# The first group's expert layer laid between the second group's attention steps, in an order written out by hand

## The reference

```
h = token(x, mask, rel_dist)            # embeddings, masked neighbour sums, norm, silu, two weights
h = h + attention(layernorm(h))         # phases, cosines and sines, cumulative sums over the tokens
h = h + experts(layernorm(h))

def experts(x):                         # E = 8 experts, the best K = 2 of each token are summed
    gate_scores = x @ Wg + bg
    _, idx = top_k(gate_scores, 2)
    mask = one_hot(idx, E).sum(-2)
    h = gelu(einsum('td,edh->teh', x, W1) + b1)     # hidden width 128
    y = einsum('teh,ehd->ted', h, W2) + b2
    return einsum('ted,te->td', y, mask)
```

## Time and profile before

| | |
|---|---|
| device time, 3 runs | 214.52, 214.59, 216.08 us; median 214.59 |
| the profiled execution: its time, its span | 213.43 us, 211.7 us |
| PE busy | 147.7 us, 70% of the span |
| PE weight loads busy | 90.8 us, 43% |
| DVE busy | 131.1 us, 62% |
| ACT busy | 73.9 us, 35% |
| POOL busy | 35.6 us, 17% |
| mean granted clock of TensorE | 0.778 of full speed |
| chain that ended last, by engine | PE 43%, DVE 34%, issue 9%, DMA 5%, ACT 5%, POOL 2% |

### The profile page before, as it was taken

How to read it: one execution, slowest core, us unless ns; L and a number is a source line. 1 busy time by engine, 2 the same in 40 slices (tenths; PEclk the granted TensorE clock), 3 DMA queues, 4 the chain that set the end, 5 groups by cost and what they waited for, 6 DMA issues and landing times.

```text
span 211.7 us, 2099 instructions
## 1 busy us (share of the span) xinstructions
PE 147.7 (70%) x690; PEld 90.8 (43%) x690; DVE 131.1 (62%) x342; ACT 73.9 (35%) x122; POOL 35.6 (17%) x52
## 2 busy tenths in 40 slices
PE   0889858029279694499581054877479989979992
PEld 0543524024175512458561053766454454534340
DVE  2659995789942898998879995388673005101011
ACT  2010511252233640784840230323063462444541
POOL 2031500346000472241402330000000000000000
PEclk9999979758857955558997555799555896799998
DMA  5999600000000000000000000000000000101011
GB/s 145 345 386 377 262 5 25 0 0 0 0 0 0 0 0 0 0 5 2 0 0 5 0 0 0 0 5 0 0 0 0 0 3 0 25 0 25 0 25 25
DMA packets 7042, 8.80 MB, mean 42 GB/s; under 512 B 2388, under 2 KB 4436, under 8 KB 7032
## 3 DMA queue, kind: packets, MB, share of 16 engines
q1 hardware_dynamic: 7032, 8.68, 12.2%
HBM read 8.15 MB, written 0.52 MB: 41 GB/s over the span
## 4 chain that ended last, share of the span: by engine, by line
PE 43%; DVE 34%; issue 9%; DMA 5%; ACT 5%; POOL 2%; SPq 1%; DVEq 0%; POOLq 0%; ACTq 0%
PE bank L900 8%; PE bank L884 6%; DMA dist_sb<-in_dist 5%; PE bank L885 4%; PE bank L861 2%; PE bank L640 2%; DVE dist_sb L988 2%; PE bank L705 2%; PE bank L698 2%; PE bank L702 2%; DVE proj L1059 2%; PE bank L707 2%; DVE invpos L993 2%; PE bank L690 2%; PE bank L754 1%
## 5 line engine op out<-in xcount | busy, mean ns | idle before, releaser
L586 ACT ACTIVATE hid<-bank 128x512 f32<-128x512 f32 x32 | 18.1, 596 | 23.3 <-PE bank L885 22.2
L900 PE MATMUL bank<-hid,ffn_sb 128*64 128x512 f32 x64 | 18.9, 676 | 0.0
L1271 DVE TENSOR_TENSOR h<-bank,h 128x256 f32<-128x256 f32 x4 | 1.7, 425 | 27.0 <-PE bank L909 27.0
L884 PE MATMUL bank<-xp,w1hi 128*128 128x512 f32 x32 | 16.6, 520 | 1.0 <-ACT xp L570 1.0
L885 PE MATMUL bank<-xp,w1lo 96*128 96x512 f32 x32 | 14.6, 455 | 0.0
L884 PEld LDWEIGHTS bank<-xp,w1hi 128*128 128x128 f32 x32 | 7.0, 220 | 14.4 <-ACT hid L586 8.1
L988 DVE TENSOR_TENSOR dist_sb<-dist_sb,mask_in 128x1024 f32<-128x1024 f32 x8 | 9.5, 1232 | 4.0 <-POOL mask_in L325 4.0
L698 PE MATMUL bank<-late_sb,proj 128*128 128x8 f32 x16 | 3.7, 364 | 10.8 <-ACT proj L469 10.8
L656 PE MATMUL bank<-early_sb,vk 128*128 128x128 f32 x8 | 2.2, 435 | 12.9 <-DVE vk L1038 12.9
L830 PE MATMUL bank<-early_sb,sq_c 128*128 128x2 f32 x16 | 2.9, 304 | 11.8 <-ACT sq_c L545 11.8
L640 PE MATMUL bank<-dist_sb,neigh 128*64 128x512 f32 x32 | 11.1, 775 | 0.0
(11 more groups left out here) (246 smaller groups left out, 369.4 us busy)
## 6 DMA issues: line engine op xcount, KB each, us to landing
dist_sb<-in_dist SPq DMA_DIRECT2D x4, 1024.0 KB, 10.8
mask_in<-in_mask SPq DMA_DIRECT2D x4, 256.0 KB, 10.0
ffn_sb<-in_ffn SPq DMA_DIRECT2D x1, 813.0 KB, 10.9
fold_sb<-in_folded SPq DMA_DIRECT2D x1, 772.0 KB, 12.1
late_sb<-in_late SPq DMA_DIRECT2D x1, 728.5 KB, 11.6
out<-h SPq DMA_DIRECT2D x8, 64.0 KB, 1.7
early_sb<-in_early SPq DMA_DIRECT2D x1, 391.0 KB, 3.2
mask_in<-in_mrows SPq DMA_DIRECT2D x1, 128.0 KB, 2.4
```

What stands on the lines that cost most here:

```text
L586: nc.scalar.activation(hid[:, at % HB], bank[hid_bank[at % 3]][:, :], ACT.Gelu).then_inc(S["hid_set"], 1)
L884: nc.tensor.matmul(o, w1hi[:, e * HID:(e + 1) * HID], xp1[g][:, toks], start=True, stop=False)
L900: mm = nc.tensor.matmul(bank[2][j * D:(j + 1) * D, :], K["e_w2"][:, (e + j) * D:(e + j + 1) * D], hid[:, (at + j) % HB], start=False, stop ...
```

## The change

It is one new order, one more empty step in X, and other banks and a later place for group 0's turns:

- `ORDER`: out3 of group 0's core, C0.8, C0.9 and X0.1 now come before or just after Q1.4 (they came after Q1.8). X0.2 and X0.3 lie between Q1.5 and Q1.7; X0.4 and X0.5 come before Q1.8. Group 0's half blocks 0 to 6 lie between the steps of group 1's core, one after each of C1.2 to C1.8. Half blocks 7 to 15 lie beside group 1's layer norm and scores; the remaining `back` of group 0 and group 1's selection come next. In the new numbering the loop over n begins at X.6.
- Each stage X has 25 steps, not 24: the selection (DVE) moved from X.3 to X.4, and the transposes of the chosen experts with their copies to X.5.
- Group 0's `turn(0)` moved from n = 12 to the last step, X0.25, where `turn(1)` is. That step now comes after the first four half blocks and the first `back` of group 1. ACT's last `copy_y` of group 0 is in this step too.
- Group 1's turns use banks 4 and 5 and no longer wait for `y_set`; group 0's turns stay in 6 and 7 and wait for group 1's attention (`state_set`) and scores (`score_read`) to be done with them.

The code gives each engine the same work as before, in another order.

```diff
-ORDER = ("T0 T0 T0 T1 T0 T1 T0 T1 T0 T0 T1 W0 T1 P0 T1 P0 T1 P0 Q0 P0 P0 Q0 P1 Q0 Q0 P1 Q0 Q0 Q0 Q0 P1 C0 "
-         "P1 P1 C0 Q1 C0 Q1 C0 C0 Q1 C0 Q1 Q1 Q1 Q1 Q1 C0 C0 C0 C1 C1 C1 C1 C1 X0 C1 X0 C1 C1 C1 X0 X1 X0 "
-         "X0 X1 X0 X0 X0 X0 X0 X0 X0 X0 X0 X0 X1 X0 X0 X1 X0 X0 X0 X0 X1 X1 X1 X0 X0 X0 X1 X1 X1 X1 X1 X1 "
-         "X1 X1 X1 X1 X1 X1 X1 X1 X1 X1 X1").split()
+ORDER = ("T0 T0 T0 T1 T0 T1 T0 T1 T0 T0 T1 W0 T1 P0 T1 P0 T1 P0 Q0 P0 P0 Q0 P1 Q0 Q0 P1 Q0 Q0 Q0 Q0 P1 C0 P1 "
+         "P1 C0 Q1 C0 Q1 C0 C0 Q1 C0 C0 Q1 C0 C0 X0 Q1 X0 Q1 X0 C1 Q1 X0 X0 Q1 C1 X0 C1 X0 C1 X0 C1 X0 C1 X0 "
+         "C1 X0 C1 X0 C1 X0 X0 X1 X0 X0 X1 X0 X0 X0 X1 X0 X0 X0 X1 X0 X0 X1 X1 X1 X1 X1 X0 X1 X1 X1 X1 X1 X1 "
+         "X1 X1 X1 X1 X1 X1 X1 X1 X1 X1").split()
...
         x_bank = (0, 4)
+        turn_bank = (6, 4)
...
             def experts(g):                      # POOL
-                yield
-                yield
-                yield
-                yield
-                for _ in range(20):
+                for _ in range(25):
                     yield
...
                     nc.scalar.copy(xp1[g][:, 512 * k:512 * k + 512], bank[x_bank[g] + k][:, :]).then_inc(S["xp1_set"], 1)
+                yield
                 yield
...
                 mm.then_inc(S["score_mm"], 1)
                 yield
+                yield
                 pe.wait_ge(S["mask_set"], g + 1)
...
                 def turn(k):
                     pe.wait_ge(S["y_copied"], 2 * g + k + 1)
-                    if g:
-                        pe.wait_ge(S["y_set"], 1 + k)
+                    if g == 0:
+                        pe.wait_ge(S["state_set"], 3 * NG)
+                        pe.wait_ge(S["score_read"], NG)
                     for c in range(4):
-                        mm = nc.tensor.transpose(bank[6 + k][:, c * P:(c + 1) * P], y_t[:, k, c * P:(c + 1) * P], ident)
+                        mm = nc.tensor.transpose(bank[turn_bank[g] + k][:, c * P:(c + 1) * P], y_t[:, k, c * P:(c + 1) * P], ident)
                     mm.then_inc(S["yt_mm"], 1)
...
-                    if n == 12:
+                    if g and n == 12:
                         turn(0)
                     yield
+                if g == 0:
+                    turn(0)
                 turn(1)
                 yield
...
                                         ALU.subtract).then_inc(S["xhl_set"], 1)
                 yield
+                yield
                 dve.wait_ge(S["score_mm"], g + 1)
...
-                    yt = bank[6 + k][:, :].rearrange("p (c j d) -> p j c d", j=2, d=D)
+                    yt = bank[turn_bank[g] + k][:, :].rearrange("p (c j d) -> p j c d", j=2, d=D)
...
                 for n in range(-1, 18):
-                    if n == 12:
+                    if g and n == 12:
                         output(0)
                     yield
+                if g == 0:
+                    output(0)
                 output(1)
                 yield
```

## The result

| | before | changed |
|---|---|---|
| device time, 4 runs each, median | 214.56 us | 207.80 us |
| lowest, highest | 213.88, 216.08 | 207.45, 208.69 |
| the profiled execution: its time, its span | 213.43, 211.7 | 207.45, 205.7 |
| mean granted clock | 0.778 | 0.807 |

The account below looks back on a forecast made before the run. It took DVE's small steps, then PE in the half blocks, as the bounds. PE from 143.5 plus 36.0 gave 179.5, plus 6.85 for clock and two turns 187.4, 3.4 earlier than 190.77: 211.2 us, range 207.4 to 214.8.

Parts of the forecast that it names:

- The clock: PE from 143.5 on: two spells at half clock, each costing half its length, add 6.85 us to the sum.
- Q1.4 to C1.2's transposes: Start of PE's stream: DVE's reordered steps from 111.75 let C1.2's transposes start at 143.5, give or take 0.7.
- two turns behind b1.0: Group 0's two turns, now behind group 1's first back, add 0.5 us each.
- The first spell: Half clock on PE from 143.5, at C1.2's transposes: 7 us long, costing 3.5 (1.95 to 5.55).
- The second spell: Half clock behind group 1's scores (X1.3), as before the change: 6.7 us long, costing 3.35 (0 to 5).
- the clock serves better: Rival: clock rises within 4 us of 143.5 or does not fall behind X1.3; typically 208 us; chance 0.16.
- The prediction's own sign of being wrong: Wrong if DVE reaches L1247 later, PE has holes in the core, or half-clock spells sum above 20 or below 8 us.
- The stream: PE from C1.2's transposes to group 1's first bias matmul (b1.0), at full clock: 36.0 us, of which the core 5.65.
- The waits: In PE's stream: 0.9 at h1.0, 1.24 for `copy_y`, some 0.5 for squares, selection nothing or at most 0.4; together 2.65 us.
- DVE's stretch: DVE from Q1.4: X0.2 ends at 129.6, new wait from 133.0 to 136.6, selection 3.60, Q1.8 3.24, to 143.4.
- The table rival: ACT: squares between gelus need another table, four loads, 5.1 us; no gain, 214.7; 0.07 of the 0.28 for gain mostly lost.
- The slower rival: PE from 143.5: mix of core and half blocks keeps half clock for 21.8 us, costing 10.9; 218.6 us; chance 0.09.

Follow-up runs that it names:

- c_warm: c_q8_turn plus 18 unread matmuls on PE while it waits for X0.2 and 3 in each copy wait ahead of the scores: 204.4 us, ratio 0.952 to before.
- a_again: The changed kernel, unaltered, run for a second trace: 206.9 us (one run).
- a_hole: Changed kernel with group 1's scores and selection moved behind h0.14, h0.15 and group 0's last two backs, leaving PE's selection wait uncovered: 213.8 us, ratio 1.005 to before.
- a_turn_early: Changed kernel with group 0's last step (copy_y, turns, outputs; X0.25) moved directly behind X0.24, ahead of X1.5: 206.7 us, ratio 0.961 to before.
- b_again: The kernel before, unaltered, run for a second trace: 211.7 us (one run).
- a_q8_first: Changed kernel with DVE's Q1.8 ahead of group 0's selection and C1.2 ahead of X0.5: 205.0 us, ratio 0.957 to before.
- c_q8_turn: Changed kernel with the moves of both a_q8_first and a_turn_early: 205.4 us, ratio 0.957 to before.
- a_core_apart: Changed kernel with group 0's half blocks 0 to 6 moved out of group 1's core to behind it: 209.8 us, ratio 0.964 to before.
- c_warm2: c_warm plus nine more unread matmuls while PE waits for group 0's selection: 205.0 us, ratio 0.964 to before.
- b_warm2: Kernel before plus eight unread matmuls in group 0's selection hole and three in the copy wait ahead of group 1's scores: 211.7 us, ratio 0.985 to before.

## Why the prediction was off

The direction, the places and nearly all waits were right; the forecast gain of 3.4 was half of the 6.8 measured. The step that failed is **"The clock"**: its two terms. They took 6.85 us for spells at half clock that cost 0.65. Set against the first trace of the kernel before, the sum's errors make 5.0 us (2.85 + 3.35 for the clock, 0.3 and 0.15 for the start and the turns, less 1.6 for the stream), 8.4 gained in place of 3.4. The medians show 6.8, since that first trace held the longer of the two spells seen behind group 1's scores.

| step of the sum (profiled execution) | forecast | measured |
|---|---|---|
| Q1.4 to C1.2's transposes | 31.75 (to 143.5) | 31.49 |
| C1.2 to b1.0, at full clock | 36.0 | 37.6 (38.26 less 0.65) |
| first spell at half clock: length, cost | 7, 3.5 | 1.3, 0.65 |
| second spell: length, cost | 6.7, 3.35 | none, 0 |
| two turns behind b1.0 | 1.0 | 0.85 |

- **The first spell** was taken to begin at 143.5 with the transposes of C1.2, because everything from there on is continuous. The clock rose at 146.97, 1.3 us after C1.2 began at 145.68. PE had by then worked from 136.07 to 145.2 with two holes, 1.84 and 0.45: scores and the transposes of C1.1 and X0.5. I counted only the work behind 143.5, as if what lay ahead did nothing for the clock; in c_warm, 18 added matmuls further ahead had the clock up at 128.88. 2.85 us. Part of this is luck: in a_again the rise came 1.1 us behind C1.2's start, but in a_hole and a_turn_early, with the same order up to there, 4.4 us behind it, which is inside the prediction's bounds (3.9 to 11.1).
- **The second spell** did not come at all, in two traces of the changed kernel of two; I had taken it over from the kernel before at 6.7. 3.35 us. In b_again it is 3.4, so even in the kernel before 6.7 was the long case. Here too there was luck: a_turn_early, with the same steps up to group 1's scores, had a spell of 3.4 us behind them, and so had a_q8_first and c_q8_turn, whose order differs only further ahead or behind. The rival "the clock serves better" is what happened, both halves of it, for 208; I gave it 0.16. The prediction's own sign of being wrong came true as well: from 143.5 on the half-clock spells sum to 3.5 us, under the 8 that it named.
- **The stream** was 1.6 us longer than summed. My 5.65 for the core, with its masks' waits covered and its ends hidden, is 6.6 by the starts of its steps: 1.0. Six half blocks that stand alone between core steps take 0.63 to 0.67 each (147.14 to 147.77, 148.42 to 149.09), where the cycle of 2.16 has 0.57: 0.5. The waits add 0.35, h1.0 to h1.3 0.2, and C1.2 and C1.8 give 0.5 back. Covering was worth less than I thought: a_core_apart lost 0.8 to 0.9, not the 2.5 of its waits.
- **The waits**: 0.35 at the bias matmul of b0.8, for the copy of bank 2 that ACT makes behind X1.1's square (0.5 forecast for squares), 0.73 for group 1's selection (0, at most 0.4), 0.72 for the copies (0.9), 1.20 for `copy_y` (1.24). The selection's cover failed because at full clock the two half blocks and two backs are over in 3.05 us.
- **DVE's stretch** came out right within 0.3, though its parts were not: X0.2 ended 18.5 after Q1.4's start, not 17.9, scores took 3.58 at half clock, not 2.86 (the 2.86 of the earlier trace rows was partly at full clock), and Q1.8 took 2.4, not 3.24.
- **The table rival** is refuted: one load. The square needs no other table than the gelu. The Trainium skill (ScalarE: Activation LUTs, "Table sets: the hidden batching unit") names copy, identity, relu and abs as the cheap functions of every set; the two squares between gelus at 158.59 and 166.14, without a load, show that here square needs none either. The load takes 1.28 and the gelu starts 1.30 behind its start, so no run here shows the drain that the same page adds ("What ACT_TABLE_LOAD costs"). **The slower rival** did not occur; a_hole shows that a long spell at half clock among the half blocks is possible, but behind a hole and not through the mix of the matmuls.

**What stays open.** Behind group 1's scores the clock fell in nine of the fourteen traces, for 3.4, 6.8 or, in a_hole, 13.7 us, and not in the changed kernel, a_again, a_core_apart, c_warm and c_warm2. Apart from the large hole of a_hole, no edit is shown to decide it: c_q8_turn and c_warm differ only in added matmuls, the changed kernel and a_q8_first only ahead of the half blocks. Both traces with three added matmuls ahead of those scores in the new order (c_warm, c_warm2) have no fall, but b_warm2, with three in the old order, has one. It is worth 1.7 to 3.4 us either way and is part of why runs of one kernel differ. I did not find what triggers it.

## What to carry to other kernels

Price a hole in TensorE's work twice: its own length, and up to half of the matmul time in the spell at half clock that follows (here 3.3 to 3.5 us for a hole of 3.63). So an order that leaves the sum of the idle time as it is, but gathers it in one stretch ahead of the dense part, can gain more than one that covers small waits. When a schedule is changed, count busy time of the same instructions before and after; where that moves, it is the clock and not the cover. And when a forecast rests on spells of the clock seen in one trace, take a second trace of the kernel before: one of mine was twice as long as in the next.

## What was not expected of the hardware

- In both traces of the changed kernel the clock stayed at full for 54 us with five waits of 0.35 to 1.21 us among the work (up to the last copy), while in a_hole one of 3.63 us, behind the scores, came with 13.7 us at half clock.
- Eight to twelve matmuls whose results nobody reads shortened a kernel by some 3 to 4 us, when they stood in such a wait; 24 or 33 of them, most ahead of work bound by DVE, brought nothing that could be measured.
- With the same work ahead of it, Q1.4 starts at 111.7 or near 114 in different traces (before: 111.75, 111.67; changed: 114.19, 113.79; c_q8_turn: 111.66). In all fourteen the early starts (111.2 to 112.1, five traces) go with one spell at half clock of 23.9 us that ends near 97, and the late ones (112.8 to 115.0, nine traces) with another pattern of spells there. That is 2.4 us and more between runs, and no edit here stands ahead of it.
